# Rotary products placed between row maxima, and the maxima's rows sent from ScalarE's queue, in a two-layer attention kernel

## What is computed

```python
# layer 1: 16 heads of 8, rotary over halves, causal softmax
q = rope(x @ Wq.T); k = rope(x @ Wk.T); v = x @ Wv.T
attn = softmax(where(causal, q @ k.T / sqrt(8), min)); out = (attn @ v) @ Wo.T
# layer 2: 16 heads of 64 = 32 plain + 32 rotary, latent keys and values of 16
q = x @ Wq; q_nope, q_rope = q[..., :32], rope(q[..., 32:])
kv_latent, k_rope = split(x @ Wkva); kv = kv_latent @ Wkvb
att = softmax(causal(concat(q_nope, q_rope) @ concat(kv, rope(k_rope)).T / sqrt(64)))
x = x + (att @ kv) @ Wo
# then a mixture of 8 experts (2 chosen) and one shared expert
```

## Time and profile before

| what | value |
|---|---|
| median of 3 runs | 642.79 us (641.87 to 645.54) |
| the profiled execution | 640.79 us, span 638.8 us |
| mean granted TensorE clock | 0.954 of 2.4 GHz |
| PE, DVE, ACT, POOL busy | 85%, 62%, 48%, 33% of the span |

### The profile page before, as it was taken

The page is one execution under the profiler, slowest core; times in us unless marked ns, Lnnn a source line. Parts: engine busy times, 40 slices in busy tenths (PEclk is TensorE's granted clock), DMA queues, the critical chain, the costliest instruction groups (busy, mean ns, idle before and its releaser), DMA issues.

```text
span 638.8 us, 9915 instructions
## 1 busy us (share of the span) xinstructions
PE 541.8 (85%) x3538; PEld 300.5 (47%) x3538; DVE 398.9 (62%) x942; ACT 307.2 (48%) x585; POOL 209.2 (33%) x273
## 2 busy tenths in 40 slices
PE   3569989888877997799878998989999998899872
PEld 1424435433444554444435555545575456643632
DVE  6588787667757554566755576756556765435463
ACT  1314666664557643456526545644445532564221
POOL 4372454333625522650442311424231110220011
PEclk9976999999889897799979999999999999999987
DMA  9660214113353450201570122216304120000000
GB/s 227 179 178 13 65 47 151 40 40 104 127 106 84 132 164 21 100 35 66 102 198 36 58 49 51 51 68 150 76 10 96 22 52 2 18 2 1 1 17 16
DMA packets 29488, 47.19 MB, mean 74 GB/s; under 512 B 4608, under 2 KB 15104, under 8 KB 28928
## 3 DMA queue, kind: packets, MB, share of 16 engines
q1 hardware_dynamic: 28480, 46.01, 27.0%
q10 hardware_dynamic: 960, 0.56, 0.4%
HBM read 27.22 MB, written 18.87 MB: 72 GB/s over the span
## 4 chain that ended last, share of the span: by engine, by line
PE 58%; DVE 20%; ACT 6%; issue 5%; POOL 4%; SPq 3%; DMA 3%; POOLq 0%; DVEq 0%; ACTq 0%
PE ps L571 12%; PE ps L528 9%; PE ps L634 8%; DVE NM L1144 6%; PE ps L499 6%; PE ps L496 4%; PE ps L501 4%; PE ps L522 3%; DVE terms L1248 2%; PE ps L756 2%; DVE stats L1128 2%; PE ps L578 2%; PE ps L682 2%; PE ps L617 1%; DVE KS L1401 1%
## 5 line engine op out<-in xcount | busy, mean ns | idle before, releaser
L1144 DVE TENSOR_REDUCE NM<-ps 128x1 f32<-128x512 f32 (+3 forms) x352 | 219.3, 638 | 118.7 <-PE ps L501 111.8
L797 ACT ACTIVATE PG<-ps 128x512 f32<-128x512 f32 x320 | 181.4, 596 | 161.2 <-PE ps L528 94.2
L528 PE MATMUL ps<-QS,K 128*128 128x512 f32 x320 | 119.4, 458 | 0.0
L501 PE MATMUL ps<-maskb,identb 128*128 128x128 bf16 x512 | 111.3, 236 | 0.0
L571 PE MATMUL ps<-PG,V 128*32 128x512 f32 (+3 forms) x1024 | 97.7, 455 | 6.9 <-POOL PG L1090 5.2
L499 PE MATMUL ps<-K,QS 96*128 96x256 f32 (+3 forms) x256 | 84.7, 375 | 15.2 <-DVE NM L1144 14.9
L496 PE MATMUL ps<-KS,QS 96*128 96x256 bf16 (+3 forms) x256 | 74.8, 328 | 20.0 <-DVE NM L1144 18.6
L501 PEld LDWEIGHTS ps<-maskb,identb 128*128 128x128 bf16 x512 | 52.8, 103 | 38.7 <-issue 31.3
L528 PEld LDWEIGHTS ps<-QS,K 128*128 128x128 f32 x320 | 51.9, 196 | 38.8 <-issue 20.3
L522 PE MATMUL ps<-QS,KS 128*128 128x128 bf16 (+3 forms) x256 | 63.9, 312 | 4.7 <-DMA QS<-scr 4.2
L988 POOL TENSOR_TENSOR rstd<-ve,half 128x4 f32<-128x4 f32 x20 | 20.5, 1023 | 139.8 <-DVE ve L1136 104.1
(11 more groups left out here) (159 smaller groups left out, 640.7 us busy)
## 6 DMA issues: line engine op xcount, KB each, us to landing
scr<-QC SPq DMA_DIRECT2D x24, 512.0 KB, 2.8
QS<-scr SPq DMA_DIRECT2D x64, 128.0 KB
...
```

What stands on the lines that cost most here:

```text
L501: return pe.matmul(dst[:, P * (k - 1):P * k], identb[:], maskb[:, 0, :], start=False, stop=True)
L528: mm = pe.matmul(bank.rearrange("p (h q) -> p h q", h=HG), keys[:, SEQ[n] % 2, P * j:P * j + P], QS2[:, heads, P * i:P * i + P], start=(ke ...
L797: act.activation(PG[:, n % 2, unit_place(LAYER[n], (u + k) % UNITS), :], ps[:, ST0 + (u + k) % 3, :], ACT.Exp, scale=scale).then_inc(exp_d ...
L1144: dve.tensor_reduce(dst, src, AX.X, ALU.max, negate=True).then_inc(fill_read, 1)
```

## The change

It has four parts. First, the four products of each `ropeA` pair are no longer a stage of their own on DVE: `rope_product` does product i right behind maximum i in `main` of the slot after the one in which PE projects the pair. Second, the DMA that sends the maxima's rows is issued by ACT, directly behind its copy, instead of by SP. Third, entries of the table move: the second `qabs` part of batch 0 before slot (8, 0) and of batch 3 before (23, 2), with batch 0's `kst2` from (7, 3) to (8, 0); batch 1's rotary stages later by two slots; `ropeB` part 2 of batches 0 and 2 one slot later. Fourth, batch 3's `parts1` goes from (10, 3) to (10, 2).

```diff
-    plan += prep1(3, ((9, 1), (9, 2), (9, 3), (10, 0), (10, 1), (10, 3), (11, 0)))
+    plan += prep1(3, ((9, 1), (9, 2), (9, 3), (10, 0), (10, 1), (10, 2), (11, 0)))
...
-                ((12, 3), "qabs", 1), ((12, 3), "kst2", 0), ((13, 0), "ropeA", 0), ((13, 0), "ropeA", 1), ((13, 1), "ropeB", 0), ((13, 2), "ropeB", 1),
+                ((12, 3), "qabs", 1), ((12, 3), "kst2", 0), ((13, 2), "ropeA", 0), ((13, 2), "ropeA", 1), ((13, 3), "ropeB", 0), ((14, 0), "ropeB", 1),
...
+ROPE_AT = {}
+for _n, _hh, _stage, _b, _part in BESIDE:
+    if _stage == "ropeA" and _part % 2 == 0:
+        ROPE_AT[divmod(HG * _n + _hh + 1, HG)] = (_b, _part)
...
...
                 act.wait_ge(m_copied, m + 1)
                 act.sem_inc(bank_read[bank_of(BANK0["turnmax", m, 0])], 1)
+                g = m % G
+                if LAYER[m] == 1:
+                    act.dma_start(QS1[MROW:MROW + 3, HG * g:HG * g + HG, :],
+                                  MP[:, m % 2, 0:T // 2].bitcast(BF16)).then_inc(m_stacked[g], 16)
+                else:
+                    act.dma_start(QS2[MROW:MROW + 2, HG * g:HG * g + HG, :].bitcast(F32),
+                                  MP[0:2 * HG, m % 2, :]).then_inc(m_stacked[g], 16)
...
+            def rope_product(b, part, i):
+                u, (second, k) = BANK0["ropeA", b, part], divmod(i, 2)
+                j, bank = JOB0["ropeA", b, part + second], u + (1 - k if second else k)
+                if k == 0 and j >= 2:
+                    dve.wait_ge(job_done[j % 2], j // 2)
+                last = dve.tensor_tensor(terms[:, j % 2, k, :], full(bank), ropeq_sb[:, k, :], ALU.mult)
+                if second:
+                    last.then_inc(bank_read[bank_of(bank)], 1)
+                    if k == 1:
+                        dve.wait_ge(*was_read(u))
+                        dve.sem_inc(terms_ready, 1)
+                elif k == 1:
+                    last.then_inc(terms_ready, 1)
...
                     if n + 2 < NG and i < 2 + hh % 2 + hh // 3:
                         maximum(n + 2, hh, i)
+                    if (n, hh) in ROPE_AT:
+                        rope_product(*ROPE_AT[n, hh], i)
```

More of the change, by code:

```diff
@@ L107, in beside @@
     plan += row(0, ((5, 0), "o1T", 0), ((5, 1), "o1y", 0), ((6, 0), "lna", 0), ((6, 2), "lna2", 0), ((7, 0), "lnb", 0),
-                ((7, 1), "x2T", 0), ((7, 2), "kst", 0), ((7, 2), "latv", 0), ((7, 3), "qabs", 0), ((7, 3), "kst2", 0),
-                ((8, 0), "qabs", 1), ((8, 0), "ropeA", 0), ((8, 0), "ropeA", 1), ((8, 1), "ropeB", 0), ((8, 2), "ropeB", 1),
-                ((8, 2), "ropeA", 2), ((8, 2), "ropeA", 3), ((8, 3), "ropeB", 2), ((9, 0), "ropeB", 3), ((9, 1), "load2", 0), ((9, 3), "load2", 1), ((10, 2), "load2", 2),
+                ((7, 1), "x2T", 0), ((7, 2), "kst", 0), ((7, 2), "latv", 0), ((7, 3), "qabs", 0), ((7, 3), "qabs", 1),
+                ((8, 0), "kst2", 0), ((8, 0), "ropeA", 0), ((8, 0), "ropeA", 1), ((8, 1), "ropeB", 0), ((8, 2), "ropeB", 1),
+                ((8, 2), "ropeA", 2), ((8, 2), "ropeA", 3), ((9, 0), "ropeB", 2), ((9, 0), "ropeB", 3), ((9, 1), "load2", 0), ((9, 3), "load2", 1), ((10, 2), "load2", 2),
                 ((11, 2), "load2", 3))
-    plan += prep1(3, ((9, 1), (9, 2), (9, 3), (10, 0), (10, 1), (10, 3), (11, 0)))
+    plan += prep1(3, ((9, 1), (9, 2), (9, 3), (10, 0), (10, 1), (10, 2), (11, 0)))
     plan += row(3, ((10, 2), "v1", 0), ((12, 2), "v1c", 0))
@@ L122, in beside @@
                 ((16, 2), "latv", 0), ((16, 2), "kst2", 0), ((17, 0), "ropeA", 0), ((17, 0), "ropeA", 1), ((17, 1), "ropeB", 0), ((17, 2), "ropeB", 1),
-                ((17, 2), "ropeA", 2), ((17, 2), "ropeA", 3), ((17, 3), "ropeB", 2), ((18, 0), "ropeB", 3), ((21, 0), "load2", 0), ((22, 0), "load2", 1),
+                ((17, 2), "ropeA", 2), ((17, 2), "ropeA", 3), ((18, 0), "ropeB", 2), ((18, 0), "ropeB", 3), ((21, 0), "load2", 0), ((22, 0), "load2", 1),
                 ((23, 0), "load2", 2), ((24, 0), "load2", 3))
@@ L130, in beside @@
     plan += row(3, ((21, 0), "o1T", 0), ((21, 1), "o1y", 0), ((21, 3), "lna", 0), ((22, 1), "lna2", 0), ((22, 3), "lnb", 0),
-                ((23, 0), "x2T", 0), ((23, 1), "qabs", 0), ((23, 2), "qabs", 1), ((23, 2), "ropeA", 0), ((23, 2), "ropeA", 1), ((23, 3), "ropeB", 0), ((24, 0), "ropeB", 1),
+                ((23, 0), "x2T", 0), ((23, 1), "qabs", 0), ((23, 1), "qabs", 1), ((23, 2), "ropeA", 0), ((23, 2), "ropeA", 1), ((23, 3), "ropeB", 0), ((24, 0), "ropeB", 1),
                 ((24, 0), "ropeA", 2), ((24, 0), "ropeA", 3), ((24, 1), "ropeB", 2),
@@ L406, in _ @@
                 sp.dma_start(dst, src).then_inc(loaded, 16)
-            def turnmax(m, _):
-                g = m % G
-                sp.wait_ge(m_copied, m + 1)
-                if LAYER[m] == 1:
-                    sp.dma_start(QS1[MROW:MROW + 3, HG * g:HG * g + HG, :],
-                                 MP[:, m % 2, 0:T // 2].bitcast(BF16)).then_inc(m_stacked[g], 16)
-                else:
-                    sp.dma_start(QS2[MROW:MROW + 2, HG * g:HG * g + HG, :].bitcast(F32),
-                                 MP[0:2 * HG, m % 2, :]).then_inc(m_stacked[g], 16)
             def ln1(b, _):
@@ L484, in fin @@
                 sp.dma_start(out_seq[b], xs[b][:]).then_inc(out_sent, 16)
-            stream(lambda n, hh: None, dict(turnmax=turnmax, ln1=ln1, store1=store1, load1=load1, qabs=store2("qabs"), ropeB=store2("ropeB"),
+            stream(lambda n, hh: None, dict(ln1=ln1, store1=store1, load1=load1, qabs=store2("qabs"), ropeB=store2("ropeB"),
                               load2=load2, experts_in=experts_in, fin=fin))
@@ L1289, in ln1n @@
                     last.then_inc(xn_ready, 1)
-            def ropeA(b, part):
-                rotation_of_pair(BANK0["ropeA", b, part - part % 2], JOB0["ropeA", b, part], part % 2 == 1, ropeq_sb)
             def wprod(b, _):
```

6 lines of the change are left out of this document (3 added, 3 removed).

## The result

| | median | range | ratio to before (95% interval) |
|---|---|---|---|
| before, 20 runs | 642.62 us | 640.59 to 645.54 | |
| the change, 20 runs | 646.54 us | 641.57 to 908.41 | 1.0049 (1.0028 to 1.0069) |
| the change again, beside the experiments (12 runs) | 647.19 us | 643.06 to 651.79 | 1.0064 (1.0034 to 1.0094) |

The forecast was 631.5 us, range 623 to 641. The change is slower by 3 to 4 us, or 0.5%. That it is not faster is clear; whether it lies past my bound of 646.0 for "slower" is not, since the interval of the ratio runs from 644.4 to 647.1 us. Two of the 20 executions of the change ran at a held-down clock (700.05 us at 0.729, the profiled one, and 908.41 us at 0.808), so the ratio leaves them out and the profile after is that of the repeated run: 647.46 us, span 645.7, clock 0.946.

The account below looks back on a forecast made before the run. PE sets the pace, losing time to waits at rotary pairs and slow clock behind them. 1.8 + 7.0 + 3.5 + 1.5 (`parts1`) - 1.5 - 1.0 = 11.3 us off 640.8 gives 629.5; median 631.5 us, range 623 to 641.

Parts of the forecast that it names:

- The sends: ACT's 32 issues, 22.8 us of new time: 1.0 us lost outside batch 3, plus 0.7 in batch 3.
- ACT's queue sets the pace: Rival: every send delays exponentials PE waits on, 652.6 us; a loss once 13.0 us are on the path; chance 0.11.
- Batch 0: `qabs` and (8, 3) waits and clock, less `turnmax` and pace: 4.6 us, of which 1.8 pass the load wait.
- Batch 2: Waits, one clock dip and earlier `ropeB` stores, less `turnmax` and pace: 3.5 us gained, between 0 and 6.2.
- The 1 us that I had put beside it: Batch 2's gain by the skill's rule: stores land as late as before, leaving about 1 us from interleaving.
- The pace in (8, 3) and (17, 3): Third and fourth fill at DVE's pace: 0.6 us; 1.1 in (17, 3) with what remains of ACT's wait.
- Short waits still cost clock: Rival: each `turnmax` wait of 1.6 us brings a clock dip of 1.7, 6.8 more, 638.3 us; chance 0.06.
- The change cancels out: Rival: products were hidden except in three slots; `turnmax` waits and pace take these back, about 642 us; chance 0.09.
- Half is given back: Rival: gains of batches 1 and 2 meet the next latency; 5 to 6 us remain, 637 us; chance 0.12.
- Waits ahead of `turnmax`: PE waits 1.6 us for the fourth product's bank in each of (8, 1), (14, 1), (17, 1), (24, 1).
- Batch 1: Transpose 0.5, (13, 3) wait 3.7 and clock 4.4 gained, less 1.6 at `turnmax`: 7.0 us.
- Batch 3: 1.6 lost at `turnmax` in (24, 1), 0.7 by the send, 0.8 back in (23, 3): 1.5 us lost.

Follow-up runs that it names:

- the best version: The change with sends on SP, third and fourth product of each pair exchanged, and `load2` of batches 0 and 1 earlier: 628.67 us; with ACT's sends 641.70.
- Experiments 3 and 7: Kernel before with only the sends moved to ACT: directly behind the copy, 650.76 us; behind the exponentials of slot (m-1, 2), 647.68 us.
- experiment 9: The change with sends on SP and exchanged last two products, plus batch 0's first `load2` moved from (9, 1) to (8, 3): 629.38 us.
- experiment 10: The change with sends on SP and exchanged last two products, plus batch 1's four `load2` moved earlier, from between batch 2's stores: 633.78 us.
- experiment 6: The change with sends on SP, and the third and fourth product of each pair exchanged: 634.49 us.
- experiments 11 and 13: The change with sends on SP and `load2` of batches 0 and 1 earlier: products interleaved, last two exchanged, 628.67 us; products in one piece, 625.67 us.
- Experiment 16: The best version with the second pairs of batches 0 and 2 projected in (9, 0) and (18, 0), not (8, 2) and (17, 2): 617.47 us.
- experiment 5: Kernel before with the change's table alone, products in one piece, sends on SP: 637.87 us.
- experiment 2: The change with the sends of the maxima's rows back in SP's queue: 639.29 us.

## Why the prediction was wrong

**The sends: the step that failed first.** I took 1.7 us of 22.8 (1.0, and 0.7 in batch 3) because ACT waits 161 us ahead of exponentials and three score banks lie between ACT and PE. Measured: 8.0 and 7.9 us, 13.0 on the best version. A sum of waits over the span says nothing of the slots in which ACT is the one that is late. The rival "ACT's queue sets the pace" named the mechanism and put the turn at 13.0 us because it counted 13.0 us of other gains, of which 3.5 were there. Experiments 3 and 7 show what I had not priced, the drain ahead of the send. The sign of being wrong that I had named, exponentials released late behind sends, is there in the change, if in few places: 3.9 us in six waits at layer 1's scores.

**Batch 0: 4.6 forecast ahead of the load wait, none found.** The 2.35 us at `qabs` went, but 1.83 came at `turnmax`; the 2.74 in (8, 3) became 2.12; a wait of 1.09 us for `xT` at the start became 2.19 in the change; and the clock from group 8's copy to group 10's is 0.95 before and in the change, so that no dip was won back. PE reached the load wait 44.4 us behind group 8's copy, where it had been 42.2. The step on the load itself held in part: it was issued 36.0 us behind that copy and not 37.6, so 1.6 us earlier for the 1.8 that I had reckoned. But PE was released 10.5 us behind the issue in place of 8.9, with two stores of 512 KB issued 2.0 us ahead of it; whether these made it slower was not isolated. With sends on SP it is issued at 39.8, behind the send of group 10. So the load wait did not take the gain, as I had said; it wasn't there. What experiment 9 wins by moving the load comes on top: it takes 36.0 us from group 8 to 10, as before.

**Batch 2: 3.5 forecast, 2.6 to 3.1 lost.** I said that without SP's sends the first ACT wait goes and the second stays in part. The first did go in the change, and the second grew to 7.41. Batch 1's load groups, not the sends, keep the stores back: with those moved in experiment 10, the waits went. But that is the smaller part. The stretch from 17 to 20 then is still 0.8 us longer than before, where experiment 6 has 2.4. It is the interleaving that I had priced too low: on one and the same table it is 0.7 us longer than before with it and 2.9 shorter in one piece (experiments 11 and 13), 3.6 us, with the clock over the stretch at 0.90 against 0.93. The Trainium skill's rule, DMA: Bandwidth & Descriptors, section Issuing engines are not separate DMA queues, is that a second issuer saves only issuing time. The trace agrees in direction, with the wait of 7.41 us. The 1 us that I had put beside it was nearer than my 3.5, but had the wrong sign too.

**The pace in (8, 3) and (17, 3): 0.6 and (with the rest of ACT's wait) 1.1 forecast, 2.12 and 2.00 us.** Four maxima and four products are 5.3 us of DVE; I spread that over fills, but PE stands in one wait. The clock falls around it in experiment 11 (0.79 over 168 to 176, against 1.00 in experiment 16). Experiment 16, 11.2 us, makes this a dear term, though it moves the stores behind the pairs too, and the two were not separated.

**The rivals.** *Short waits still cost clock* is open in the small: behind the first `turnmax` wait the clock of the change was 1.00 over 164 to 172, with sends on SP 0.79 over 156 to 164. *The change cancels out* (642) is nearest to what the change is without its sends (639.3). *Half is given back* names load and store waits; the store waits are 1.6 us of batch 2's miss, the load wait did not grow.

**Right.** Waits ahead of `turnmax`: 1.6 forecast, 1.83 and three of 1.50. Batch 1: 7.0 forecast, 7.4 and 6.7, with the clock at 1.00 where it was 0.68; experiment 5 has 3.4 of it from the table alone. Batch 3: 0.8 loss without its send, 1.2 measured with sends on SP; with them on ACT it is 4.7. The load wait of about 4 us: 4.00 in experiment 2, but 2.11 in the change, where PE came to it 5.0 us later than before and the load landed only 2.8 later. "The rows themselves arrive no earlier" held too; they even arrive later, as with PE's wait of 1.09 us for them at 220.06.

**Of the sum,** -11.3 forecast and +6.9 found between the two profiles, 18.2 us are missed: the sends are 6.3 of it (8.0 for 1.7), and, read with the sends on SP, batch 0 is 4.8 (3.0 lost for 1.8 won) and batch 2 is 6.6 (3.1 for 3.5). The small terms and the ends add up to 0.5. In the medians the miss is 15.0, because the profiled execution of before was 2.0 us under its median and that of the change 0.9 us over its own.
